# One power instruction on GpSimd for every norm's inverse root, in a two-layer decoder kernel on one core

## The reference, cut to what matters

```python
def _layernorm(x, axis=-1, eps=1e-05):
    m = jnp.mean(x, axis=axis, keepdims=True)
    v = jnp.var(x, axis=axis, keepdims=True)
    return (x - m) / jnp.sqrt(v + eps)
...
        Rn = (Rg - mu) * jax.lax.rsqrt(var + EPS)      # group norm: one group per head of 16
```

## Time and profile before

| what | value |
|---|---|
| time, median of 3 runs | 1781.63 us (1781.4 to 1788.87) |
| the profiled execution's own time | 1784.68 us |
| its span in the trace | 1782.9 us |
| TensorE busy, share of the span | 1575.3 us, 88% |
| VectorE busy | 1020.5 us, 57% |
| ScalarE busy | 599.9 us, 34% |
| GpSimd busy | 409.7 us, 23% |
| mean granted TensorE clock | 0.942 of full speed |

### The profile page before, as it was taken

The page is one execution under the profiler, slowest core; times in us unless marked ns, Lnnn a source line. Parts: engine busy times, 40 slices in busy tenths (PEclk is TensorE's granted clock), DMA queues, the critical chain, the costliest instruction groups (busy, mean ns, idle before and its releaser), DMA issues. The chain is left out here.

```text
span 1782.9 us, 29275 instructions
## 1 busy us (share of the span) xinstructions
PE 1575.3 (88%) x9415; PEld 1050.6 (59%) x9416; DVE 1020.5 (57%) x2024; ACT 599.9 (34%) x1167; POOL 409.7 (23%) x839
## 2 busy tenths in 40 slices
PE   6899999999969961699999999969998938999996
PEld 5433333333346740577777777736556627999996
DVE  6778888888639967411122111168889964444443
ACT  3267777777735530111111111123336610000000
POOL 1000000000013410324222211136653312333332
PEclk9799999999989975799999999979999968999998
DMA  2112221111320120132233331110006115666664
GB/s 74 40 36 60 56 58 37 43 40 42 112 78 13 37 75 4 45 89 48 74 92 100 100 86 15 13 51 2 1 2 213 37 60 170 180 182 180 193 176 117
DMA packets 89222, 134.90 MB, mean 76 GB/s; under 512 B 17712, under 2 KB 66224, under 8 KB 88976
## 3 DMA queue, kind: packets, MB, share of 16 engines
q1 hardware_dynamic: 73968, 113.08, 20.2%
q0 software_dynamic: 15168, 20.72, 7.3%
HBM read 98.04 MB, written 20.84 MB: 67 GB/s over the span
## 5 line engine op out<-in xcount | busy, mean ns | idle before, releaser
L2111 DVE TENSOR_REDUCE mx<-ps 128x1 f32<-128x1024 f32 x256 | 306.2, 1217 | 58.6 <-PE ps L2220 58.5
L2010 ACT ACTIVATE turns_of_use<-ps 128x512 f32<-128x512 f32 x512 | 281.5, 596 | 132.1 <-PE ps L2227 130.0
L1295 PE MATMUL ps<-xTe,wide 128*128 128x320 f32 x1024 | 279.4, 435 | 1.0 <-issue 1.0
L1295 PEld LDWEIGHTS ps<-xTe,wide 128*128 128x128 f32 x1024 | 195.5, 191 | 82.1 <-issue 2.5
L1362 DVE TENSOR_TENSOR hTe<-prT,ps 128x320 f32<-128x320 f32 x128 | 62.5, 488 | 214.3 <-ACT prT L1334 209.0
L2227 PE MATMUL ps<-QS,KS 99*128 99x512 bf16 x512 | 163.7, 388 | 6.9 <-ACT turns_of_use L2010 4.7
L507 POOL TENSOR_TENSOR nv<-nv 128x2 f32<-128x2 f32 (+2 forms) x84 | 17.7, 211 | 616.4 <-DVE nv L698 612.0
L2220 PE MATMUL ps<-KS,QS 96*128 96x512 bf16 x512 | 145.1, 397 | 9.8 <-DVE mx L2111 6.9
L1452 PEld LDWEIGHTS ps<-xw_all,w1t 128*128 128x128 f32 x1248 | 145.8, 192 | 3.8 <-issue 1.0
L1452 PE MATMUL ps<-xw_all,w1t 128*128 128x128 f32 x1248 | 146.3, 276 | 1.3 <-ACT xw_all L1484 1.3
L1334 ACT ACTIVATE prT<-ps 128x320 f32<-128x320 f32 x128 | 56.0, 437 | 264.4 <-PE ps L1295 255.9
(11 more groups left out here) (313 smaller groups left out, 2139.3 us busy)
## 6 DMA issues: line engine op xcount, KB each, us to landing
w1t<-in_L_ffn_w SPq DMA_DIRECT2D x39, 1024.0 KB
wide<-in_L_ffn_gate_weight SPq DMA_DIRECT2D x8, 1024.0 KB
wide<-_L_ffn_ff_pre_act_weight SPq DMA_DIRECT2D x8, 1024.0 KB
wide<-L_ffn_ff_post_act_weight SPq DMA_DIRECT2D x8, 1024.0 KB
wide<-in_L_ffn_w SPq DMA_DIRECT2D x1, 8192.0 KB, 27.2
QS<-wide SPq DMA_DIRECT2D x192, 32.0 KB, 2.0
KS<-wide SPq DMA_DIRECT2D x192, 32.0 KB, 2.0
VS<-V_all SPq DMA_DIRECT2D x32, 128.0 KB, 2.1
```

What stands on the lines that cost most here:

```text
L1295: ins = pe.matmul(ps[:, 3 + 2 * (q % 2) + n, 0:HC], wt[:, k, f * P:f * P + P], xTe[:, k, hf * HC:hf * HC + HC], start=(k == 0), stop=(k == ...
L2010: act.activation(PT[:, q % 8, :], ps[:, 4 + q % 2, :], ACT.Exp).then_inc(h_e.sem, 1)
L2111: v.tensor_reduce(mx[:, s, t:t + 1], ps[:, 2 * (t % 2):2 * (t % 2) + 2, :], AX.XY, ALU.max).then_inc(h_rm.sem, 1)
```

## The change

GpSimd gets two constant tiles, `root` (-0.5) and `eps`. `begin_factors` on VectorE ends with the aggregation of the statistics. `finish_factors` on GpSimd adds epsilon, takes the power -0.5 in one `tensor_tensor` with `ALU.pow`, and makes the factors as before. In the group norm VectorE writes variance plus epsilon in one instruction, and GpSimd takes the power over 16 columns in one instruction. In retention the iterations that were spread over several tiles go, and the two batches of factors are made in one piece at tiles 1 and 10.

```diff
-        three_halves = sb("three_halves", [P, H])
+        root = sb("root", [P, H])
+        eps = sb("eps", [P, 1])
...
-        def begin_factors(v, c, t0, t1, done):
+        def begin_factors(v, t0, t1, done):
             for t in range(t0, t1):
                 ins = v.bn_aggr(mv[:, t, :], stats[:, t, :])
-            c(ins)
-            cols = slice(t0, t1)
-            c(v.tensor_scalar(nv[:, 2, cols], mv[:, cols, 1], float(LN_EPS), -0.5, ALU.add, ALU.mult))
-            c(v.tensor_scalar(nv[:, 1, cols].bitcast(I32), nv[:, 2, cols].bitcast(I32), 1, None, ALU.logical_shift_right))
-            v.tensor_scalar(nv[:, 0, cols].bitcast(I32), nv[:, 1, cols].bitcast(I32), -1.0,
-                            float(0x5F3759DF + 0x3FC00000), ALU.mult, ALU.add).then_inc(done.sem, 1)
+            ins.then_inc(done.sem, 1)
...
         def finish_factors(pool, c, t0, t1, done):
-            cols = slice(t0, t1)
-            n4 = nv[:, :, cols]
-            c(pool.tensor_tensor(n4[:, 0], n4[:, 0], n4[:, 1], ALU.mult))
-            c(pool.tensor_tensor(n4[:, 3], mv[:, cols, 0], n4[:, 0], ALU.mult))
-            pool.tensor_tensor(nmr[:, cols], zeros[:, 0:1].to_broadcast([P, t1 - t0]), n4[:, 3], ALU.subtract)\
+            cols, n = slice(t0, t1), t1 - t0
+            c(pool.tensor_tensor(nv[:, 2, cols], mv[:, cols, 1], eps[:].to_broadcast([P, n]), ALU.add))
+            c(pool.tensor_tensor(nv[:, 0, cols], nv[:, 2, cols], root[:, 0:n], ALU.pow))
+            c(pool.tensor_tensor(nv[:, 3, cols], mv[:, cols, 0], nv[:, 0, cols], ALU.mult))
+            pool.tensor_tensor(nmr[:, cols], zeros[:, 0:1].to_broadcast([P, n]), nv[:, 3, cols], ALU.subtract)\
                 .then_inc(done.sem, 1)
 
         def end_factors(pool, c, u, begun, done, step):
             pool.wait_ge(begun.sem, begun.upto(step))
-            newton(pool, c, nv[:, :, 2 * u:2 * u + 2])
             finish_factors(pool, c, 2 * u, 2 * u + 2, done)
...
-                newton(pool, c, gnv)
-                pool.tensor_tensor(gnv[:, 0, :], gnv[:, 0, :], gnv[:, 1, :], ALU.mult).then_inc(e_gr.sem, 1)
+                pool.tensor_tensor(gnv[:, 0, :], gnv[:, 1, :], root[:], ALU.pow).then_inc(e_gr.sem, 1)
...
                 if i == 1:
                     pool.wait_ge(x_fia.sem, x_fia.upto(NP + 1))
-                if 1 <= i <= 3:
-                    newton_round(pool, c, back, i == 3)
-                if i == 4:
                     finish_factors(pool, c, *BACK[2], e_fa)
-                if i == 9:
+                if i == 10:
                     pool.wait_ge(x_fia.sem, x_fia.upto(NP + 2))
-                if 9 <= i <= 11:
-                    newton_round(pool, c, batch0, i == 11)
-                if i == 12:
                     finish_factors(pool, c, 0, TB, x_fa)
```

More of the change, by code:

```diff
@@ L354, in decoder @@
         gscale = sbR("gscale", [P, KC, P])
-        gnv = sbR("gnv", [P, 4, 16])
+        gnv = sbR("gnv", [P, 2, 16])
         oTR = sbR("oTR", [P, KC, P])
@@ L500, in rsqrt @@
                 c(v.scalar_tensor_tensor(out=y, in0=g, scalar=1.5, in1=y, op0=ALU.add, op1=ALU.mult))
[L502 to L516, removed]
         def transpose_rows(pe, u, s, bank, xn_sig, xt_sig, tr_sig):
@@ L737, in factors @@
                 c(row_stats(v, 2 * u, 2))
-                begin_factors(v, c, 2 * u, 2 * u + 2, done)
+                begin_factors(v, 2 * u, 2 * u + 2, done)
             def keep_logits(u, U):
@@ L1739, in variances @@
                 v.wait_ge(e_gv.sem, e_gv.upto(t, 1))
[L1740 to L1745, removed]
+                v.tensor_scalar(gnv[:, 1, :].rearrange("p (c n) -> p c n", n=4),
+                                gsum[:].rearrange("p (c r) -> p c r", r=32)[:, :, 0:4], float(DH * LN_EPS),
+                                1.0 / DH, ALU.add, ALU.mult).then_inc(e_gv.sem, 1)
             def added(t):
@@ L1753, in added @@
                 if t % TB == TB - 1:
-                    begin_factors(v, c, t + 1 - TB, t + 1, x_fia)
+                    begin_factors(v, t + 1 - TB, t + 1, x_fia)
             v.memset(spaced[:].rearrange("p s j a d -> p (s j a d)"), 0.0).then_inc(e_w, 1)
@@ L1768, in dve_retention @@
                 if i == -1:
-                    begin_factors(v, c, *BACK[1], x_fia)
+                    begin_factors(v, *BACK[1], x_fia)
                     rows_back(2)
-                    begin_factors(v, c, *BACK[2], x_fia)
+                    begin_factors(v, *BACK[2], x_fia)
                 if on(i - 1):
@@ L1843, in pool_retention @@
             pool.wait_ge(e_w, 3)
-            batch0, back = nv[:, :, 0:TB], nv[:, :, BACK[2][0]:BACK[2][1]]
             for i in range(-1, NT):
@@ L1867, in pool_retention @@
                     pool.wait_ge(x_fia.sem, x_fia.upto(NP))
-                    newton(pool, c, nv[:, :, BACK[1][0]:BACK[1][1]])
                     finish_factors(pool, c, *BACK[1], e_fa)
             pool.wait_ge(x_fia.sem, x_fia.upto(NP + 3))
-            newton(pool, c, nv[:, :, TB:NT])
             finish_factors(pool, c, TB, NT, x_fa)
@@ L1949, in _ @@
             c(pool.memset(onesb[:], 1.0))
-            c(pool.memset(three_halves[:], 1.5))
+            c(pool.memset(root[:], -0.5))
+            c(pool.memset(eps[:], LN_EPS))
             pool.memset(KS[96:99, :, :].rearrange("p n s -> p (n s)").bitcast(F32), TWO_ONES).then_inc(ones_set, 1)
```

## The result

The changed kernel takes 1771.3 us (median of 6 runs, 1767.09 to 1773.99) beside 1786.0 us for the kernel before (6 runs, 1781.4 to 1788.87): 14.7 us between the medians. The recorded ratio, which is not just that of the two medians, is 0.9914, 95% interval 0.9891 to 0.9937, so 15.4 us less, with 11 to 19 us possible. The forecast was 16.6 us less, and 1765 us on a scale on which the kernel before stood at 1781.63; on that scale the ratio gives 1766.3 us. The profiled execution took 1767.09 us, the shortest of the six, and its span is 1764.4 us, 18.5 less than before.

A forecast was written before the change was run, and what follows sets the result against it. It took a ring through VectorE and TensorE to bound the cross-attention loops, TensorE retention's tiles, and exposed chains the ends. Terms summed to 16.6 us, 1784.68 to 1768.1 profiled, so 1765 us for the median, range 1760 to 1776.

The forecast's parts named there:

- loop of cross 0: Cross attention 0: first guess off VectorE gains 0.6 us in steps 1 to 6, plus 0.4 in the first two: 4.0 us.
- loop of cross 1: Cross attention 1: first guess off VectorE gains 0.6 us in each of steps 1 to 6: 3.6 us.
- end of cross 0: Last pair of cross attention 0: statistics to ScalarE's use falls from 4.92 to 1.3 us, gain 3.6 us.
- end of cross 1: Last pair of cross attention 1: statistics to ScalarE's use falls from 4.56 to 1.3 us, gain 3.2 us.
- start of cross 0: ScalarE's first use also waits for VectorE's set-up, so only three guess instructions ahead of it count: 0.5 us.
- retention: Steady tiles gain 0; one tile after half the rows 0.4, first softmax after retention 0.7, guess for eight tiles 0.6: 1.7 us.
- the ring: Cross 0's loop: TensorE, VectorE's addition, statistics, guess, softmax, logits, TensorE again; one guess group per step lies on it.
- the prediction's sign: What would show the forecast in cross attention 0: steps of 14.74 us down to 14.1.
- Price of the power: GpSimd's power taken as twice the replaced operations, 0.05 us a column: 0.3 us for 2 columns, 1.0 for 16.
- rival C: Retention: power chains over 4.8 us lengthen 14 tiles, break-even 6.0 us; at the upper bound 34 us slower, 1815 us; chance 0.14.
- Drain: GpSimd's 6.47 us drain ending cross attention 1 keeps its length and moves with the work, so the whole 3.2 us stay.
- rival A: Start of cross 0: first power comes 6.4 us late, leaving 13.6 us gained, 1768 us; chance 0.06.

The follow-up runs named there:

- Experiments 1 to 4: experiment 1, experiment 2, experiment 3, and a fourth: the changed kernel with retention's group norm iterated as before, 1772.29 us, ratio 0.9924 to the kernel before.
- experiment 1: Changed kernel with three small VectorE instructions, as long as the removed guess, behind every group but the last pair's in both cross attentions: 1778.36 us, ratio 0.9957.
- experiment 2: Changed kernel with those three VectorE instructions in cross attention 0 only, behind the earlier attention's pairs alone: 1770.37 us, ratio 0.9926.
- experiment 3: Changed kernel with the last pair's factors of each cross attention made as before, guess on VectorE and iteration on GpSimd: 1778.77 us, ratio 0.9954.

## Why the prediction was right, and which terms were off

| term | forecast | in the traces |
|---|---|---|
| loop of cross 0 | 4.0 | 2.6 |
| loop of cross 1 | 3.6 | 3.7 |
| end of cross 0 | 3.6 | 3.2 |
| end of cross 1 | 3.2 | 2.9 |
| start of cross 0 | 0.5 | 0.7 |
| retention | 1.7 | 1.7 (0.4 + 0.7 + 0.6) |
| sum | 16.6 | 14.8 |

The start of cross 0 is 517.79 - 513.33 = 4.46 us from the statistics to ScalarE's use, instead of 5.19. The sum of 14.8 us stands beside a measured 15.4 (11 to 19), or 14.7 by the medians. Experiments 1 to 4 took out the two loops, the two ends, the start of cross 0 and the 0.7 of retention one by one; the other two terms of retention are read from the profiles of before and after alone.

**Loop of cross 0.** The step that failed: "so I count 0.6 us" for each of six steps. The mechanism was right (the guess behind the residual addition is on the ring, experiment 1; the other one isn't, experiment 2), and what failed is that the softmax behind it has a second input. In the kernel before:

```profile
612.32 1.13 PE L889 MATMUL ps<-Kbd,qT 64*128 64x256 f32 x8
...
1380.53 1.13 PE L889 MATMUL ps<-Kbd,qT 64*128 64x256 f32 x8
...
1382.48 1.23 DVE L712 TENSOR_TENSOR ps<-ps,mask_f 128x1024 f32<-128x1024 f32 x1
```

In cross 0 TensorE's scores started at 612.32 and took 1.13, so they were there at 613.45, and the softmax started at 613.89: 0.44 us of slack, less the handover. Hence 0.37 a step, and steps of 14.37 us where the prediction's sign was 14.1. In cross 1 the slack was 0.8 us (1381.66 to 1382.48) and the whole 0.62 came. The row of the scores stood in the same stretch of the trace as the rows quoted, and I did not look past the ring. At the end of retention I did look, and that term came out at 0.7 as forecast.

**Price of the power.** "I take twice, 0.05 us a column": it is 0.16, plus 0.39 to start. The ends lost 0.4 and 0.3 us of their gain to it, and nothing more, since in retention it is covered. The argument for the low end, that GpSimd's simple operations cost nearly the same for 2 and 16 columns, was half good: partitions are indeed worked on side by side (32 cost what 128 do), but columns follow one another, and a multiplication's 0.002 us a column says nothing about a power's. The upper bound of 0.5 was the honest part. It gave rival C its chance of 0.14, and C's mechanism held up: beyond a window of 4.9 us GpSimd sets the tile. Its break-even, a chain of 6.0 us, came out as well (5.89 us measured 0.9999), but that number is in part luck, since errors cancel: a tile grew by 0.56 us instead of the excess of 1.1, and against that stand the end of retention, late by 3.15 us, which the break-even left out, and a gain that was smaller than 16.6 us.

**Drain.** Taken as a fixed length, and the argument was thin (another drain of nearly the same length). The changed kernel and experiment 3 have it at 6.469 us, from two other starts, and VectorE's routing waits for it in both.

**The rest.** The first use (rival A) costs nothing, twice. Retention's steady tiles gained nothing, as forecast. Of the half microsecond of the earlier trace rows 0.4 came back, as forecast, from the row norms' part that used to be spread over those tiles. The profiled span moved by 18.5 us, 3.7 more than the terms. The last pair of cross 0 makes 4.3 and the last pair of cross 1 takes 1.7 back; from the first rotation of retention to the second it is 1.3 less, at a mean granted clock of 0.83 instead of 0.72; the rest, of both signs, lies up to the first steps of cross 0 and in the two expert stages, and I have not taken it apart.

## What to carry to other kernels

When an instruction leaves a ring, list every input of the instruction behind it, with the time at which each is ready: the gain of a step is at most the smallest slack, even where more time than that was removed. An operation with no row of its own needs a break-even price worked out from the cover (here 4.9 us); then only the side of it on which the price falls matters, and one small run can measure both. The parts of this edit with most instructions were worth least: twelve to one in every tile of retention gave 0.7 us, two short chains in the open at the ends of the cross attentions gave 6.1.

## What the runs showed of the hardware that I had not expected

A power on GpSimd costs about 0.39 us and 0.16 us for each column, the same for the exponents -0.5 and 2 and for 32 and 128 partitions: some 76 times a multiplication for each column, so it is cheap for 2 columns (0.70 us beside eleven links of 0.27) and would be dear for a row of 256 (by these figures an estimate of 41 us; the longest measured is 20.8 us for 128). GpSimd's drain behind cross attention 1 takes 6.469 us in every kernel of which I read it, while the shortest of the three at that line takes 0.034 and the median one 0.041; what its length is made of no run here shows. And the same instructions between two additions of cross 0's last pairs took from 9.55 to 12.43 us in seven profiled executions with the same code there, by TensorE's granted clock alone: a difference between two profiles has to be taken stretch by stretch before a cause is given for it.
